# Sixteen tiles of a routed expert layer fixed from five blocks' counts, and the gate product from f16 halves

## The reference

```python
# layer 1: a gated recurrence, 4 heads of 64
g  = (layernorm(x) @ W_in.T) @ W_gate.T + b_gate        # 1024 gates a token: i, f, o, c per head
c  = sigmoid(f) * c + exp(i) * tanh(c_t)                # along the 256 tokens of a sequence
h  = sigmoid(o) * tanh(c * rsqrt(mean(c*c) + EPS) * rms_w)
x  = x + layernorm(h @ W_out.T)
# layer 2: 16 experts, 4 for each token
l  = layernorm(x) @ router_weight.T + router_bias
w  = softmax over the 4 largest of l, 0 elsewhere
gate, up = layernorm(x) @ gate_up_proj[e] + bias        # 256 -> 256 and 256, gate at most 7, up clipped to +-7
y  = sum_e w_e * (((up + 1) * gate * sigmoid(1.702 * gate)) @ down_proj[e] + bias)
x  = x + layernorm(y)
```

## Time and profile before

| what | value |
|---|---|
| median of three runs | 798.14 us |
| profiled execution, its span | 802.32 us, 800.5 us |
| mean granted TensorE clock | 0.859 |
| busy: TensorE | 635.2 us, 79% |
| busy: VectorE | 537.2 us, 67% |
| busy: ScalarE | 458.7 us, 57% |
| busy: GpSimd | 396.1 us, 49% |

### The profile page before, as it was taken

How to read it: one execution, slowest core, us unless ns; L and a number is a source line. 1 busy time by engine, 2 the same in 40 slices (tenths; PEclk the granted TensorE clock), 3 DMA queues, 4 the chain that set the end, 5 groups by cost and what they waited for, 6 DMA issues and landing times.

```text
span 800.5 us, 13282 instructions
## 1 busy us (share of the span) xinstructions
PE 635.2 (79%) x3658; PEld 408.9 (51%) x3658; DVE 537.2 (67%) x1570; ACT 458.7 (57%) x933; POOL 396.1 (49%) x300
## 2 busy tenths in 40 slices
PE   5887979598998752302999999999999999997450
PEld 2344636264565541201666666666666666664230
DVE  3637487778878978500777777777777777771892
ACT  2777686547546533101666767767767767762242
POOL 0012214654845737752466666666666656565121
PEclk9979798889989856555999999999999999997555
DMA  7966754799522223253677777776777676645987
GB/s 250 423 238 106 150 92 71 224 318 347 158 86 101 89 72 119 106 207 99 112 114 110 111 113 111 108 114 109 113 113 114 108 114 102 108 58 76 350 149 102
DMA packets 111895, 115.35 MB, mean 144 GB/s; under 512 B 31730, under 2 KB 101506, under 8 KB 110162
## 3 DMA queue, kind: packets, MB, share of 16 engines
q0 software_dynamic: 35456, 50.35, 37.2%
q1 hardware_dynamic: 76370, 64.16, 26.7%
HBM read 55.15 MB, written 59.31 MB: 143 GB/s over the span
## 4 chain that ended last, share of the span: by engine, by line
PE 59%; DVE 12%; DMA 8%; POOL 7%; ACT 6%; issue 5%; SPq 2%; POOLq 0%; ACTq 0%; DVEq 0%
PE PS L633 8%; PE PS L634 8%; PE PS L635 8%; PE PS L502 7%; POOL routed L916 6%; PE PS L624 4%; PE PS L653 4%; PE PS L641 4%; PE PS L654 4%; PE PS L655 4%; PE PS L525 2%; PE PS L533 2%; DMA W<-w_dn 2%; DMA W<-neg_mem 1%; DVE small L1325 1%
## 5 line engine op out<-in xcount | busy, mean ns | idle before, releaser
L942 POOL DMA_INDIRECT sums<-arena x144 | 223.2, 1550 | 143.8 <-ACT arena L702 71.5
L916 POOL DMA_INDIRECT routed<-arena,small x128 | 142.7, 1115 | 90.6 <-DVE small L1162 45.3
L1303 DVE TENSOR_SCALAR arena<-PS,small 128x256 f32<-128x256 f32 x144 | 78.3, 544 | 126.7 <-ACT arena L875 124.7
L702 ACT ACTIVATE arena<-PS 128x512 f16<-128x512 f16 (+1 forms) x180 | 105.1, 589 | 78.7 <-PE PS L624 45.7
L502 PE MATMUL PS<-arena 128*128 128x512 f32 x256 | 134.0, 668 | 10.7 <-ACT arena L702 10.6
L875 ACT ACTIVATE arena<-PS,small 128x256 f32<-128x256 f32 x144 | 68.1, 473 | 104.1 <-PE PS L635 104.1
L633 PE MATMUL PS<-W,arena 128*128 x288 | 110.2, 382 | 0.0
L634 PE MATMUL PS<-W,arena 128*128 x288 | 110.1, 382 | 0.0
L635 PE MATMUL PS<-W,arena 128*128 x288 | 109.9, 382 | 0.0
L502 PEld LDWEIGHTS PS<-arena 128*128 128x128 f32 x256 | 51.9, 214 | 69.3 <-issue 65.8
L624 PE MATMUL PS<-ident,arena 128*128 128x128 f16 x576 | 56.3, 221 | 36.7 <-DMA arena<-routed 35.9
(11 more groups left out here) (164 smaller groups left out, 1023.3 us busy)
## 6 DMA issues: line engine op xcount, KB each, us to landing
arena<-routed SPq DMA_DIRECT2D x144, 128.0 KB
W<-w_gu SPq DMA_DIRECT2D x8, 1024.0 KB, 23.6
W<-neg_mem POOLq DMA_DIRECT2D x16, 512.0 KB, 8.5
sums<-zero SPq DMA_DIRECT2D x2, 4096.0 KB, 26.2
W<-sums SPq DMA_DIRECT2D x16, 512.0 KB, 8.8
X<-x SPq DMA_DIRECT2D x8, 512.0 KB, 4.8
W<-w_dn SPq DMA_DIRECT2D x4, 1024.0 KB, 11.4
out<-X SPq DMA_DIRECT2D x8, 512.0 KB, 3.0
```

Of the source, the lines that this page charges most:

```text
L702: return nc.scalar.activation(o, i, ACT.Copy, **kw)
L916: pool.indirect_dma_start(routed, bass.IndirectOffsetOnAxis(ap=idx, axis=0), rows[b][:, jk // TOPK, :], None).then_inc(rows_sent[lane], 16)
L942: pool.indirect_dma_start(sums[j % SUMS], bass.IndirectOffsetOnAxis(ap=dst[j % MU], axis=0), yb[u], None, compute_op=ALU.add).then_inc(y_s ...
L1303: L.send(v.tensor_scalar(up[j % 2], acc[:, FF:2 * FF], gu_hi, gu_lo, ALU.min, ALU.max))
```

## The change

(1) **Early tiles.** The counts of blocks 0 to 4 (EARLY_AT = 4) fix a first table of 16 full tiles (EARLY = 16). VectorE computes it at the end of step 7 with everything spread over partitions (table_cols(0), left_over), TensorE turns it to rows in step 8 (table_rows(0)), VectorE writes the integers (table_ints(0)). SyncE may load those tiles' rows when the scatters of blocks 0 to 4 are through. The second table (128 tiles, from the rest) is made at tiles 1 to 4; pads and the wait for all scatters stand before tile 16. GpSimd's queue is as before. The first 16 tiles use two PSUM banks for gate_up, so each waits for the activation of two tiles before.

(2) **Gates from halves.** WcT and xT are kept as f16 high and low halves: WcT gets a power of two as scale from its maximum, ScalarE writes its high halves, VectorE its low ones, at the start. evac_x writes the high half of x, x_low on VectorE the low one, after y_norm of the step. Each gate chunk is six f16 matmuls.

(3) **The norm of y.** The mean is taken out of W_out once, so y has mean 0. Its squares are summed on ScalarE (square_y, after chunk 6) in place of norm_y; VectorE's y_stats becomes one small operation that waits for them, and residual reads y from PSUM with its scale, four operations.

```diff
+EARLY = 16
+EARLY_AT = 4
+COUNT_AT = 1
+LATE = TILES - EARLY
...
+        def part(j):
+
+            return (0, j, EARLY - j) if j < EARLY else (1, j - EARLY, TILES - j)
+
+        def acc_bank(j):
+
+            return j % 2 if j < EARLY else (j - EARLY + 2) % 3
-                    known += held(tab_e, E - 1, name, len(known), min(HELD, TILES - len(known)))
+                    h, at, left = part(len(known))
+                    if at == 0:
+                        eng.wait_ge(tab_ready, h + 1)
+                    known += held(tab_e[h], E - 1, name, at, min(HELD, left))
...
-            sp.wait_ge(tab_ready, 1)
-            pad = K[:, C_PAD - DIM:C_SPARE]
-            first = held(tab_pad, E * REGION - P, mybir.EngineType.SP, 0, E)
-            for e in range(E):
-                sp.dma_start(routed[ds(first[e], P), :], pad).then_inc(pad_sent, 16)
-            sp.wait_ge(pad_sent, 16 * (E + 2))
-            for b in range(2):
-                sp.wait_ge(rows_sent[b], 16 * BT * TOPK * NBLK // 2)
-
+            def pads():
+                pad = K[:, C_PAD - DIM:C_SPARE]
+                first = held(tab_pad, E * REGION - P, mybir.EngineType.SP, 0, E)
+                for e in range(E):
+                    sp.dma_start(routed[ds(first[e], P), :], pad).then_inc(pad_sent, 16)
+                sp.wait_ge(pad_sent, 16 * (E + 2))
+
+            sp.wait_ge(gate_mm, NBLK * CHUNKS)
             rows_at, pairs_at = [], []
             for j in range(TILES):
+                h, at, left = part(j)
+                if at == 0:
+                    sp.wait_ge(tab_ready, h + 1)
+                    if h:
+                        pads()
+                    for lane in range(2):
+                        sp.wait_ge(rows_sent[lane], 16 * (BT * TOPK // 2) * (NBLK if h else EARLY_AT + 1))
                 if len(rows_at) == j:
...
             def gates(t, c):
                 if t or c >= 2:
                     pe.wait_ge(gate_act, 8 * t + (c - 1))
+                if c == 0:
+                    pe.wait_ge(xT_ready, KT * (t + 1))
+                    pe.wait_ge(xl_ready, KT * (t + 1))
+                if t == 0 and c % (CHUNKS // 2) == 0:
+                    pe.wait_ge(wc_low, KT * (c // (CHUNKS // 2) + 1))
                 for k in range(KT):
-                    if c == 0:
-                        pe.wait_ge(xT_ready, 2 * t + (k + 1))
-                    last = mm(PS[:, 2 + c % 2, :], WcT[:, k, c * P:(c + 1) * P], xT[:, k, :],
-                              start=(k == 0), stop=(k == KT - 1))
+                    whi, wlo = [WcT[:, h, k, c * P:(c + 1) * P] for h in range(2)]
+                    mm(PS[:, 2 + c % 2, :], whi, xT[:, 0, k, :], start=(k == 0), stop=False)
+                    mm(PS[:, 2 + c % 2, :], whi, xT[:, 1, k, :], start=False, stop=False)
...
+                if t == EARLY_AT:
+                    mm(PS[:, 7, 448:448 + E], oneB, before[:, :], start=True, stop=False)
+                    mm(PS[:, 7, 448:448 + E], oneB, chosen[:, 0, :], start=False, stop=False)
+                    for j in range(1, BT):
+                        mm(PS[:, 7, 448:448 + E], oneB, chosen[:, j, :], start=False, stop=(j == BT - 1))
...
+            def table_rows(h):
+                pe.wait_ge(cols_ready, h + 1)
+                n = LATE if h else EARLY
+                for i in range(2):
+                    last = mm(PS[0:1, 2, P + i * P:P + i * P + n], cols[:, i:i + 1], K[:, C_IDENT:C_IDENT + n],
+                              start=True, stop=True)
+                last.then_inc(tab_mm, 1)
 
             def step(s):
                 new, mid, old = on(s, 0), on(s, 1), on(s, 2)
                 for c in range(CHUNKS):
+                    if (s, c) == (NBLK, 2):
+                        table_rows(0)
...
@@ pe, after the last step @@
-            pe.wait_ge(before_ready, NBLK + 1)
-            mm(PS[0:1, 0, 0:E], KB[:, B_ONE:B_ONE + 1], before[:, :], start=True, stop=True)
-            mm(PS[0:E, 1, 0:1], before[:, :], KB[:, B_ONE:B_ONE + 1], start=True, stop=True).then_inc(cnt_mm, 1)
-            pe.wait_ge(nt_ready, 1)
-            mm(PS[0:E, 2, 0:1], K[0:E, C_TRI16:C_TRI16 + E], nt_col, start=True, stop=True).then_inc(end_mm, 1)
-            pe.wait_ge(cmp_ready, 1)
-            mm(PS[0:1, 3, 0:TILES], K[0:E, C_TRI16 + E - 1:C_TRI16 + E], ended, start=True, stop=True)
-            mm(PS[0:1, 4, 0:TILES], dl_col, ended, start=True, stop=True).then_inc(tab_mm, 1)
-
-
-            pe.wait_ge(tab_ready, 1)
...
-                acc = PS[:, j % 3, :]
+                acc = PS[:, acc_bank(j), :]
                 pe.wait_ge(xq_ready, j + 1)
+                if 2 <= j < EARLY:
+                    pe.wait_ge(act_ready, j - 1)
...
+                if j == COUNT_AT:
+                    pe.wait_ge(before_ready, NBLK + 1)
+                    mm(PS[:, 2, 0:E], oneB, before[:, :], start=True, stop=True).then_inc(cnt_mm, 1)
+                if j == COUNT_AT + 3:
+                    table_rows(1)
...
-            def norm_y(t):
-                act.wait_ge(r2_ready, t + 1)
+            def square_y(t):
+                act.wait_ge(y_mm, t + 1)
                 if t:
                     act.wait_ge(log_mm, t)
                 for j in range(BT):
                     last = nc.scalar.activation(yn[:, j, :], PS[:, 4 + j // 2, (j % 2) * DIM:(j % 2 + 1) * DIM],
-                                                ACT.Identity, bias=mr2[:, j:j + 1], scale=r2[:, j:j + 1])
-                last.then_inc(yn_ready, 1)
+                                                ACT.Square, accum_out=ysq[:, j:j + 1])
+                last.then_inc(ysq_ready, 1)
...
-                    if c == CHUNKS - 1 and mid:
-                        norm_y(s - 1)
+                    if c == CHUNKS - 2 and mid:
+                        square_y(s - 1)
...
+            act.wait_ge(wc_scaled, 1)
+            for n in range(2):
+                for m in range(KT):
+                    copy(WcT[:, 0, m, n * 512:(n + 1) * 512], PS[:, 4 + 2 * n + m, :], scale=wc_scale).then_inc(wc_high, 1)
...
@@ dve @@
+            for i in range(2 * KT):
+                dve.wait_ge(wc_mm, i + 1)
+                last = v.tensor_reduce(wc_peak[:, i:i + 1], PS[:, 4 + i, :], AX, ALU.max, apply_absolute_value=True)
+            L(last)
+            L(v.tensor_reduce(peak, wc_peak, AX, ALU.max))
+            v.tensor_copy(spread, peak.to_broadcast([P, P])).then_inc(peak_ready, 1)
+            dve.wait_ge(peak_mm, 1)
+            L(v.tensor_reduce(peak_all, PS[:, 2, 0:P], AX, ALU.max))
+            L(v.tensor_scalar(expo, peak_all.bitcast(i32), 23, None, ALU.logical_shift_right))
+            L(v.tensor_scalar(expo, expo, EXP_LOW, None, ALU.max))
+
+            def power(o, sign, exponent):
+                return v.tensor_scalar(o.bitcast(i32), expo, sign * 2.0 ** 23, exponent * 2.0 ** 23, ALU.mult, ALU.add)
+
+            power(wc_scale, -1, 268).then_inc(wc_scaled, 1)
+            power(g_whole, 1, -14 - X_BITS)
+            power(g_half, 1, -15 - X_BITS).then_inc(wc_scaled, 1)
+            dve.wait_ge(wc_scaled, 2)
+
+            def x_low(t):
+                for k in range(KT):
+                    dve.wait_ge(xT_ready, KT * t + k + 1)
+                    v.scalar_tensor_tensor(xT[:, 1, k, :], PS[:, k, :], float(2 ** X_BITS), xT[:, 0, k, :],
+                                           ALU.mult, ALU.subtract).then_inc(xl_ready, 1)
+
+            x_low(0)
+            for i in range(2 * KT):
+                n, m = i // KT, i % KT
+                dve.wait_ge(wc_high, i + 1)
+                v.scalar_tensor_tensor(WcT[:, 1, m, n * 512:(n + 1) * 512], PS[:, 4 + i, :], wc_scale,
+                                       WcT[:, 0, m, n * 512:(n + 1) * 512], ALU.mult, ALU.subtract).then_inc(wc_low, 1)
...
+            L(v.tensor_reduce(wo_mean, WoT, AX, ALU.add))
+            L(v.tensor_scalar(wo_mean, wo_mean, 1.0 / DIM, None, ALU.mult))
+            for q in range(PAIRS):
+                v.tensor_scalar(WoT[:, q, :], WoT[:, q, :], wo_mean[:, q:q + 1], None, ALU.subtract).then_inc(wr_ready, 1)
...
-                dve.wait_ge(yn_ready, t + 1)
-                L(v.tensor_tensor(block_x(t), block_x(t), yn, ALU.add))
+                for j in range(BT):
+                    last = v.scalar_tensor_tensor(block_x(t)[:, j, :], PS[:, 4 + j // 2, (j % 2) * DIM:(j % 2 + 1) * DIM],
+                                                  r2[:, j:j + 1], block_x(t)[:, j, :], ALU.mult, ALU.add)
+                last.then_inc(res_done, 1)
+                dve.wait_ge(res_done, t + 1)
...
-                dve.wait_ge(y_mm, t + 1)
-                stats(lambda j: PS[:, 4 + j // 2, (j % 2) * DIM:(j % 2 + 1) * DIM], mv2, 4 * LN_EPS)
-
-            def y_norm(done=r2_ready):
+                dve.wait_ge(ysq_ready, t + 1)
+                L(v.tensor_scalar(nv[:, 0:BT], ysq, 1.0 / DIM, 4 * LN_EPS, ALU.mult, ALU.add))
...
+            def table_cols(h):
+
+                full = mstep[:, :]
```

(42 more changed lines are left out.)

124 lines of the change are left out of this document (60 added, 64 removed).

## The result

The changed kernel takes **822.15 us**, the median of four runs (816.48 to 824.16), against 798.50 us of the kernel before in its four (797.46 to 801.88): ratio 1.0277, interval 1.0217 to 1.0337. Its profiled execution took 821.55 us with a span of 819.7, 19.2 more than the 802.32 and 800.5 of before.

A forecast was written before the change was run, and what follows sets the result against it. VectorE was taken to bound most attention steps, GpSimd's two write lanes the expert part. Terms +32.9 + 3 − 17.6 − 7.4, with 0.5 for pads and table loads, gave +11.5: 813.8 profiled, 810 us forecast, range 794 to 826.

The forecast's parts named there:

- the 5.9 worked out: Attention step 5: VectorE arrives at 204.3, ScalarE's squares are done at 210.2, so VectorE stands 5.9 us.
- the third rival: Attention part: TensorE's clock falls as it stands; spread and output product lose 1.5 us in seven steps; 820 us, chance 0.15.
- Start-up: Before step 1: preparing W_c and WoT on VectorE, and squares of w_dn, delay the start by 4.5 us (bounds 2 and 8).
- Steps: Attention steps 2 to 7 lengthen by 20.5 us in all, step 8 by 4.4, plus 3.5 for the table.
- steps 5 and 7 +4.4 each: Attention steps where VectorE bounds: wait for squares, x_low and longer residual end each 4.4 us later.
- The pieces: Single operations: two x_low 1.3 us, residual about 1.5, table 3.5, six-matmul gate chunk 1.28, ScalarE's squares 2.7.
- Last scatters: GpSimd: scatter(7) and the end of scatter(6) share time with tile work and lose about 3 us.
- First write: GpSimd: the first accumulating write comes at the last scatter's landing, 2.5 us after its issue, near 403 to 406.
- 17.6 less: Expert part: early tiles save at most the pipe's filling, first write near 369.5 instead of 387.10 before other delays.
- Lane rate: Expert part: GpSimd's two write lanes set the pace at 2.37 us a tile, 7.4 us less over 143 intervals.
- the gates' saving: Gate product on TensorE: 0.43 us a chunk, 27.5 in all, if the step waits for TensorE; in step 5 it does not.
- the fourth rival: Last two scatters: each issue is held by a VectorE operation of tile work, 15 us instead of 3; 822 us, chance 0.05.

The follow-up runs named there:

- A alone: Kernel before plus only the early table and early tiles, gates in f32 and norm of y as before: 787.79 us, ratio 0.9819.
- B alone: Kernel before plus only the gate product from f16 halves, with two semaphores of the final table merged: 813.42 us, ratio 1.0126.

## Why the prediction was right, and where it was not

Forecast 810 us, slower, for the reason given: VectorE waits for the squares behind ScalarE's chunk 6. That holds: 47.8 us in eight blocks, and a reordering that fills the wait takes the loss away. That the mean of 6.0 meets the 5.9 worked out is luck in part: the waits run from 2.8 to 11.4 us, and step 5, for which 5.9 was worked out, has 4.75. The measured 822 is 12 over, on the side of the third rival. By terms:

- **Start-up** +4.5: measured 4.2 (hidden(0) at 62.27 against 58.10).
- **Steps.** Forecast for steps 2 to 8: 2.9, 4.9, 2.1, 4.4, 1.8, 4.4 and 7.9 with the table. Measured, from the start of hidden(s-2) to that of hidden(s-1) for step s: 3.0, 4.5, 4.3, **9.6**, 3.2, 4.7 and 8.0. Each of these stretches holds the wait for squares that stands in step s-1. The term mis-sized is "steps 5 and 7 +4.4 each", in step 5, then step 4. These terms took TensorE's work at its speed of before. Logits and output product between hidden(3) and the squares took 9.5 us in place of 5.6, so the squares began 3.9 later. The sum to slots(5) was 41.5 instead of 32.9.
- **Which waits count.** The forecast put the wait of step 8 into slots(5), and none for step 1. The trace has it the other way: slots(5), at 336.48, stands ahead of step 8's wait (to 347.65) and behind step 1's, the longest (11.44). Seven waits stand ahead of it either way, so the slip shows little in the sum.
- **The pieces.** x_low 1.29 (1.3), residual 1.63 (1.5), table 3.75 in A alone (3.5), a chunk at the high level 1.29 (1.28). The squares take about 1.5 us, not 2.7: a pass and its read need 0.35 together (starts at 196.03 and 196.38). In step 5 that alone takes the wait from 5.9 to near the 4.75 measured. In step 4, where they also started late, the two errors offset each other in part, and the wait is 7.11.
- **Rival 3, the clock**, had chance 0.15 and 820 us, and was no alternative to the forecast but came on top. Its 1.5 us a step for spread and output product was too low: in steps 4 and 5 they lost 1.73 and 2.33, and the logits 1.58, which it left out. The idle matmuls put the whole at about 11 us.
- **Last scatters** +3 for VectorE's tile work beside them: measured 2 less, 69.5 us from first to last against 71.6. The 5.1 us between forecast and measurement hid part of what the steps cost more, which was luck.
- **First write.** The landing took 3.33 us from the last issue (409.74), not 2.5. "17.6 less" for the filling holds otherwise (16.8).
- **Lane rate**, "2.37 each": measured 2.401, so 2.9 us less than before, not 7.4. The stretch I took (505 to 586) was one of the faster ones, and it was not the lanes' own: in it TensorE was busy throughout and each write followed its copy closely (1.35 us at tile 64). So it does not show the lanes' rate.
- The differences, 8.6 for the steps - 5.1 for the scatters + 0.8 + 4.5 - 1.0 for pads and tail, are 7.8 with rounding, the 7.7 us between 11.5 and 19.2. The rest of the 12 is how the medians lie to the profiled executions: the forecast took off 4.2 us, but the changed kernel's profiled execution lay at its median.

That the gates' saving goes to waste is shown: B alone costs 1.3%. That the early tiles pay for little more than the filling is shown too: A alone gains 1.8%, 13 us, its first write comes 13.4 us earlier and its last 15.8, and the store of tiles is still there at the last write.

## What to carry to other kernels

Moving an operation to an engine with time to spare puts it at a place in that engine's order; look at what stands ahead of it, and who stands waiting meanwhile. Where a wait can't be removed, put independent work of the waiting engine ahead of it, and mend one order at a time. When TensorE comes to wait in more places, price all its work behind the waits at the lower clock, not one operation of it. A queue with a store in front of it sets the pace only if it is slower than what fills the store; compare the lag of its writes at two tiles before giving it the time.

## What the runs showed of the hardware

TensorE's granted clock from 80 to 320 was 0.83 before, 0.76 with the change and 0.84 with idle matmuls in two of its stands, with the same real work, and the kernel was some 11 us shorter by it. With the gates from halves and the old norm of y (ab) it was 0.75, so the squares are not what lowers it.

The scatters beside tile work were not slower: of the last 16 (from 385.07 to 406.41) all took 0.97 us but one of 1.23, while VectorE was busy 7.20 of the 10 us from 390 to 400; the mean over 128 went from 1.115 to 1.058. Of the four VectorE operations of a tile only one, line 1411, has both tensor inputs in SBUF. From 390 to 400 it starts at 390.21, 392.79, 395.18, 397.58 and 399.98, each time while an issue runs, and each of those five issues took 0.97 us. The Trainium skill (SBUF — State Buffer, "Who interferes with whom") has a VectorE operation with two SBUF inputs contend with a GpSimd instruction that reads SBUF; it also infers that making descriptors needs the write interface, of which a tensor_tensor takes nothing. The five issues agree with the second, and the fourth rival, which went by the first alone, is out.

Why TensorE and ScalarE stood 5 to 9 us at a time on one chip stays open.
